# Near keys of the maximum pass: two units of 128-query windows become one unit of 64-query halves in four 64x64 tiles of the array

## The reference, cut to what matters

```python
def _strided_allowed(S):
    i = jnp.arange(S)[:, None]
    j = jnp.arange(S)[None, :]
    return (j % STRIDE == 0) | (jnp.abs(i - j) <= LOCAL)      # STRIDE 4, LOCAL 8
...
scores = jnp.einsum('bhqd,bhkd->bhqk', q, k) / jnp.sqrt(D)
scores = jnp.where(allowed, scores, -jnp.inf)
attn = jax.nn.softmax(scores, axis=-1)
out = jnp.einsum('bhqk,bhkd->bhqd', attn, v)
```

## Time and profile before

| what | value |
|---|---|
| median of 3 runs | 1088.07 us (1084.07 to 1089.80) |
| profiled execution, own time | 1086.01 us |
| its span, first to last instruction | 1084.2 us |
| PE / DVE / ACT / POOL busy | 95% / 86% / 77% / 23% of the span |
| mean granted clock of TensorE | 0.987 |
| chain that ended last | PE 76%, DVE 12%, issue 7% |

### The profile page before, as it was taken

The page is one execution under the profiler, slowest core; times in us unless marked ns, Lnnn a source line. Parts: engine busy times, 40 slices in busy tenths (PEclk is TensorE's granted clock), DMA queues, the critical chain, the costliest instruction groups (busy, mean ns, idle before and its releaser), DMA issues.

```text
span 1084.2 us, 27687 instructions
## 1 busy us (share of the span) xinstructions
PE 1028.3 (95%) x10694; PEld 462.7 (43%) x10695; DVE 933.8 (86%) x1162; ACT 839.8 (77%) x1590; POOL 251.2 (23%) x387
## 2 busy tenths in 40 slices
PE   4999999699999999999999999999999999999898
PEld 2666666233333333333333333333333333333487
DVE  6989897889999999999999999999999999999133
ACT  4667674288888888888888888888888888888600
POOL 2444453012212121221212122212121222212100
PEclk9999999599999999999999999999999999999999
DMA  6787878213223333333333333323343332231166
GB/s 197 227 254 252 262 250 274 54 46 88 85 83 90 98 85 93 102 91 99 97 96 109 98 99 95 104 84 108 91 113 88 105 91 82 86 85 58 48 236 239
DMA packets 166777, 134.07 MB, mean 124 GB/s; under 512 B 70492, under 2 KB 145884, under 8 KB 166636
## 3 DMA queue, kind: packets, MB, share of 16 engines
q1 hardware_dynamic: 163912, 128.06, 39.3%
q10 hardware_dynamic: 2736, 4.26, 1.2%
HBM read 71.13 MB, written 59.84 MB: 121 GB/s over the span
## 4 chain that ended last, share of the span: by engine, by line
PE 76%; DVE 12%; issue 7%; DMA 2%; ACT 2%; DVEq 0%; ACTq 0%
PE ps_attend L1228 17%; PE ps_attend L1145 12%; DVE peak_far L1087 10%; PE ps_attend L1186 10%; PE ps_project L621 7%; PE ps_attend L1235 6%; PE ps_attend L1308 5%; PE ps_attend L1156 4%; PE ps_project L679 4%; PE ps_attend L1197 3%; PE ps_project L594 3%; PE ps_attend L1163 3%; PE ps_attend L1204 2%; DMA sums<-out_rows 2%; PE ps_project L656 1%
## 5 line engine op out<-in xcount | busy, mean ns | idle before, releaser
L1087 DVE TENSOR_REDUCE peak_far<-ps_attend 128x2 f32<-128x1024 f32 x512 | 608.5, 1220 | 41.0 <-PE ps_attend L1186 30.8
L1028 ACT ACTIVATE probs<-ps_attend 128x512 f32<-128x512 f32 x1024 | 541.1, 597 | 49.5 <-PE ps_attend L1145 46.3
L1228 PE MATMUL ps_attend<-probs,v_op 128*17 128x512 f32 x2048 | 270.1, 600 | 0.5 <-issue 0.5
L1145 PE MATMUL ps_attend<-q_op,k_op 51*128 51x512 f16 x1024 | 252.1, 387 | 4.9 <-ACT probs L1028 3.3
L1186 PE MATMUL ps_attend<-k_op,q_op 48*128 48x512 f16 x1024 | 189.6, 388 | 26.1 <-DVE peak_far L1087 15.5
L1033 ACT ACTIVATE probs<-ps_attend 108x512 f32<-108x512 f32 x256 | 138.7, 594 | 34.6 <-PE ps_attend L1163 34.6
L1145 PEld LDWEIGHTS ps_attend<-q_op,k_op 51*128 51x128 f16 x1024 | 76.8, 93 | 193.9 <-ACT probs L1028 137.4
L894 POOL CAST negmax<-peak 128x16 bf16<-128x16 f32 x64 | 12.6, 196 | 609.6 <-DVE peak L1070 609.6
L1090 DVE TENSOR_REDUCE peak_near<-ps_attend 128x8 f32<-128x864 f32 x128 | 131.0, 1023 | 10.5 <-PE ps_attend L1204 10.4
L885 POOL TENSOR_TENSOR out_rows<-out_rows,share_rows 128x512 f32<-128x512 f32 x64 | 81.4, 1272 | 66.1 <-DMA share_rows<-shares_dram 64.0
L621 PE MATMUL ps_project<-xT_parts,w_parts 128*128 128x512 f16 x384 | 90.6, 387 | 2.1 <-DVE xT_parts L465 2.1
(11 more groups left out here) (91 smaller groups left out, 937.4 us busy)
## 6 DMA issues: line engine op xcount, KB each, us to landing
share_rows<-shares_dram SPq DMA_DIRECT2D x64, 256.0 KB
attn_dram<-out_rows SPq DMA_DIRECT2D x64, 256.0 KB, 5.5
q_dram<-qk_parts SPq DMA_DIRECT2D x48, 256.0 KB, 4.7
k_dram<-qk_parts SPq DMA_DIRECT2D x48, 256.0 KB, 2.7
q_op<-q_dram SPq DMA_DIRECT2D x128, 96.0 KB, 2.4
k_op<-k_dram SPq DMA_DIRECT2D x64, 144.0 KB, 3.1
v_dram<-v_sb SPq DMA_DIRECT2D x16, 544.0 KB, 3.0
base<-in_x SPq DMA_DIRECT2D x16, 512.0 KB, 4.7
```

The lines of the kernel that those rows point to most:

```text
L1028: ins = nc.scalar.activation(probs[:, r, h], ps_s[st.bank(kind)], ACT.Exp, scale=undo)
L1087: ins = nc.vector.tensor_reduce(peak_far[:, :, p, tile], banks, AX_X, ALU.max)
L1145: nc.tensor.matmul(bank, k[half(f, KM), keys], q[half(f, KM), p], start=True, stop=True).then_inc(s_ready, 1)
L1228: ins = nc.tensor.matmul(ps_o[h * VW:h * VW + VR], v[:, r, h * VR:(h + 1) * VR], probs[:, r, h], start=(r == 0), stop=False)
```

## The change

The two near units of a step become one. Its queries come in halves of 64 and each half meets its own window of 60 keys. The two heads of a pair use the upper and lower rows of the array and the two halves of a tile its left and right columns, so four 64x64 tiles are in use. One mask, relative to the query, serves every window: per tile of the array one product of 480 columns (2 pairs x 4 tiles x 60 keys), then 32 products of 64 x 60. One DVE maximum reads 960 elements per partition and gives 16. A step has nine units; the near unit stands seventh, on PE between `maxima()` and `far(3, 1)`.

As the mask no longer knows the ends of the sequence, a window that reaches past an end must find keys there that are allowed anyway: the strided keys of the two pairs now lie side by side in the middle of `k_op`, and the 6 columns at either end get copies of strided keys from POOL, four small copies for every load of keys (`set_edges`), which PE's near unit waits for in the step before their first use. The memsets of the ends and SP's wait for them go; SP loads two new mask arrays (128x64 and 128x480 bf16) at the start. `places(u)` and `strided(u)` give the new columns.

```diff
+SUB = HALF
+NEAR = (SUB + 2 * LOCAL) // STRIDE * (STRIDE - 1)
+SUB_STEP = SUB // STRIDE * (STRIDE - 1)
+NEAR_BANDS = ((1, 16), (4, 6), (12, 5))
...
+def strided(u):
+
+    return WPAD + (S if u else S - NS)
+
+
+def places(u):
+
+    return WPAD + u * (S + NS)
...
-        at = WPAD + u * S
-        eng.dma_start(k_op[half(f), at:at + S - NS].rearrange("r (c s) -> r c s", c=CPB), rows[:, :, ns:]
-                      ).then_inc(loaded, 16)
-        eng.dma_start(k_op[half(f), at + S - NS:at + S].rearrange("r (c s) -> r c s", c=CPB), rows[:, :, 0:ns]
-                      ).then_inc(loaded, 16)
+        eng.dma_start(k_op[half(f), places(u):places(u) + S - NS].rearrange("r (c s) -> r c s", c=CPB),
+                      rows[:, :, ns:]).then_inc(loaded, 16)
+        eng.dma_start(k_op[half(f), strided(u):strided(u) + NS].rearrange("r (c s) -> r c s", c=CPB),
+                      rows[:, :, 0:ns]).then_inc(loaded, 16)
...
-            sp.wait_ge(pads_set, 4)
+            sp.dma_start(keep["near_q"][:], io["rel_q"].bitcast(BF16)).then_inc(keep["bands_loaded"], 16)
+            sp.dma_start(keep["near_k"][:], io["rel_k"].bitcast(BF16)).then_inc(keep["bands_loaded"], 16)
...
-            for par in range(2):
-                nc.gpsimd.memset(keep["k_op"][par][:, 0:WPAD], 0.0).then_inc(pads_set, 1)
-                nc.gpsimd.memset(keep["k_op"][par][:, SK - WPAD:], 0.0).then_inc(pads_set, 1)
...
-UNITS = TT * PAIRS + TT // 2
+UNITS = TT * PAIRS + 1
...
-AHEAD = 5
-TURN = 8
+AHEAD = 4
+TURN = 7
...
-    ("far", 2, 1), ("far", 1, 0), ("far", 0, 0), ("near", 0), ("far", 2, 0),
-    ("far", 3, 1), ("far", 1, 1), ("far", 3, 0), ("near", 1), ("far", 0, 1),
+    ("far", 2, 1), ("far", 1, 0), ("far", 0, 0), ("far", 2, 0),
+    ("far", 3, 1), ("far", 1, 1), ("near",), ("far", 3, 0), ("far", 0, 1),
...
     def window(p, tile):
-        return p * S + WSTEP * tile
-
-    def strided(p):
-        return WPAD + p * S + S - NS
+        return places(p) - WPAD + WSTEP * tile
...
+        def set_edges(st):
+
+            k, it = k_op[st.parity(2)], st.iteration(2)
+            pool.wait_ge(k_loaded[st.parity(2)], 16 * 2 * 2 * PAIRS * (st.half_iteration(2) + 1))
+            edges = ((0, strided(0)), (SK - WPAD, strided(1)))
+            for i, (f, (to, of)) in enumerate(itertools.product(range(2), edges)):
+                nc.gpsimd.tensor_copy(k[half(f), to:to + WPAD], k[half(f), of:of + WPAD]).then_inc(edges_ready, 1)
+                pool.wait_ge(edges_ready, 4 * it + i + 1)
+
+        pool.wait_ge(done["y8_ready"], B * CPB)
+        set_edges(Step(0, FIRST))
         pool.wait_ge(done["base_ready"], B * CPB)
-        pool.wait_ge(pads_set, 5)
+        pool.wait_ge(pads_set, 1)
...
+            if st.n >= 0 and st.exists(2) and st.queries(2) == 0:
+                pool.wait_ge(negmax_ready, st.at(2))
+                set_edges(st)
...
-                    tile = 2 * kind[1]
-                    ins = nc.vector.tensor_reduce(peak_near[:, :, tile:tile + 2].rearrange("q f t p -> q f (t p)"),
-                                                  banks[:, :, 0:2 * PAIRS * WIN].rearrange("q f (g w) -> q f g w",
-                                                                                           w=WIN), AX_X, ALU.max)
+                    ins = nc.vector.tensor_reduce(peak_near[:].rearrange("q f p t -> q f (p t)"),
+                                                  banks[:, :, 0:PAIRS * TT * NEAR].rearrange(
+                                                      "q f (g w) -> q f g w", w=NEAR), AX_X, ALU.max)
...
+            if st.queries(2) == 0:
+                pe.wait_ge(edges_ready, 4 * (st.iteration(2) + 1))
             if 2 * n + 2 > U_BANKS:
                 pe.wait_ge(u_used, 2 * n + 2 - U_BANKS)
-            for t in range(2):
-                tile = 2 * kind[1] + t
-                cols = slice(tile * P, (tile + 1) * P)
-                at_mask = close(st.queries(d) * TT + tile)
-                whole = slice(t * PAIRS * WIN, (t + 1) * PAIRS * WIN)
-                for f in range(2):
-                    nc.tensor.matmul(banks[f][:, whole].rearrange("q (p w) -> q p w", p=PAIRS),
-                                     mask_q[half(f), st.queries(d) * CH + tile * P:st.queries(d) * CH + (tile + 1) * P],
-                                     mask_k[half(f), at_mask:at_mask + WIN].unsqueeze(1).broadcast_to([KR, PAIRS, WIN]),
-                                     start=True, stop=False)
-                for p in range(PAIRS):
-                    at = window(p, st.queries(d) * TT + tile)
-                    for f in range(2):
-                        ins = nc.tensor.matmul(banks[f][:, (t * PAIRS + p) * WIN:(t * PAIRS + p + 1) * WIN],
-                                               q[half(f), p, cols], k[half(f), at:at + WIN],
-                                               start=False, stop=(p == PAIRS - 1))
-                        if t == 1 and p == PAIRS - 1:
-                            ins.then_inc(u_ready, 1)
+            for sub, f in itertools.product(range(2), range(2)):
+                nc.tensor.matmul(banks[f][half(sub, SUB), 0:PAIRS * TT * NEAR], near_q[half(f)], near_k[half(f)],
+                                 start=True, stop=False)
+            for p, t in itertools.product(range(PAIRS), range(TT)):
+                for sub, f in itertools.product(range(2), range(2)):
+                    at = window(p, st.queries(2) * TT + t) + sub * SUB_STEP
+                    to = (p * TT + t) * NEAR
+                    ins = nc.tensor.matmul(banks[f][half(sub, SUB), to:to + NEAR],
+                                           q[half(f), p, t * P + sub * SUB:t * P + (sub + 1) * SUB],
+                                           k[half(f), at:at + NEAR], start=False,
+                                           stop=(p == PAIRS - 1 and t == TT - 1))
+                    if p == PAIRS - 1 and t == TT - 1 and sub == 1:
+                        ins.then_inc(u_ready, 1)
...
             far(2, 1)
             weigh_last(3)
             far(1, 0)
-            near_unit(0)
             far_unit(2, 0)
             far(1, 1)
             weigh_last(4)
@@ -1285,9 +1304,9 @@
             far(2, 0)
             weigh_own(0)
             maxima()
+            near_unit()
             far(3, 1)
             far_unit(3, 0)
-            near_unit(1)
             far(3, 0)
             weigh_own(1)
...
+    at = np.arange(NEAR)
+    hot = np.concatenate([np.arange(n)[:, None] == at // size % n for size, n in NEAR_BANDS])
+    beside = np.abs(STRIDE * (at // 3) + 1 + at % 3 - LOCAL - np.arange(SUB)[:, None]) <= LOCAL
+    rel_k = np.zeros((2, HALF, PAIRS * TT, NEAR), np.float32)
+    rel_k[:, :len(hot)] = hot[:, None, :]
+    rel_q = np.zeros((2, HALF, SUB), np.float32)
+    rel_q[:, :len(hot)] = np.where(hot.astype(int) @ beside.T.astype(int), 0, -BIG)
```

More of the change, by code:

```diff
@@ L690, in tensor_project @@
             chunks(pe, body)
-        done = dict(f_ready=f_ready, lo_ready=lo_ready, ranges_ready=ranges_ready, v_copied=v_copied,
+        done = dict(f_ready=f_ready, y8_ready=y8_ready, lo_ready=lo_ready, ranges_ready=ranges_ready, v_copied=v_copied,
                     base_ready=base_ready, bias_ready=bias_ready, masks_ready=masks_ready, rest_loaded=rest_loaded,
@@ L815, in part_attend @@
     k_loaded = keep["k_loaded"]
+    near_q, near_k = keep["near_q"], keep["near_k"]
+    edges_ready = sem("edges_ready")
     v_loaded = [sem(f"v_loaded{i}") for i in range(2)]
@@ L1069, in maximum @@
                     dve.wait_ge(negmax_ready, st.at())
-                nc.vector.tensor_tensor(peak[:, (st.n + 1) % 2], peak_far[:],
-                                        peak_near[:].rearrange("q f t p -> q f p t"), ALU.max).then_inc(peak_ready, 1)
+                nc.vector.tensor_tensor(peak[:, (st.n + 1) % 2], peak_far[:], peak_near[:], ALU.max
+                                        ).then_inc(peak_ready, 1)
             for i, kind in enumerate(MAXIMA):
@@ L1244, in far_unit, with near_unit @@
                 unit(st, ("far", tile, p))
-            def near_unit(tiles):
-                unit(st, ("near", tiles))
+            def near_unit():
+                unit(st, ("near",))
             def far(r, p):
@@ L1311, in project @@
             last.then_inc(y_ready, 1)
-        pe.wait_ge(keep["bands_loaded"], 16 * 6)
-        pe.wait_ge(pads_set, 5)
+        pe.wait_ge(keep["bands_loaded"], 16 * 8)
+        pe.wait_ge(pads_set, 1)
         pe.wait_ge(done["masks_ready"], 1)
@@ L1353, in build @@
             "k_op": [sb(f"k_op{i}", [P, SK], F16) for i in range(2)],
+            "near_q": sb("near_q", [P, SUB], BF16),
+            "near_k": sb("near_k", [P, PAIRS * TT * NEAR], BF16),
             "v_op": sb("v_op0", [P, NS // P + S // P, HG * VR]),
@@ L1358, in build @@
             "peak_far": sb("peak_far", [P, 2, PAIRS, TT]),
-            "peak_near": sb("peak_near", [P, 2, TT, PAIRS]),
+            "peak_near": sb("peak_near", [P, 2, PAIRS, TT]),
```

(2 more changed lines are left out.)

## The result

The changed kernel takes 1114.36 us (median of 4 runs, 1114.15 to 1114.96); the kernel before, beside it, 1087.28 us. The ratio is 1.0252, 95% interval 1.0223 to 1.028: slower by 2.5%. The profiled execution took 1114.96 us, its span is 1113.1 us, 28.9 more than before.

The account below looks back on a forecast made before the run. The prediction took a closed chain of PE and ACT's read latency to bound the step, 12.59 us. From 1086.0 us, + 37.2 for the near unit, - 1 lead-in, - 2 irregular steps gave 1120 us, range 1108 to 1152.

Parts of the forecast that it names:

- a chain of PE and ACT's latency: Attend stage: PE, ACT's read and PE again set the 12.59 us step; near-unit and DVE work are not on it.
- the last step: End of the attend stage: a step without units or DVE maxima took 12.58 us and should keep that length.
- The near unit: On PE between the negated maxima and far(3, 1): adds 0.60 us in each of 62 steps, 37.2 us.
- the burst of starts in the earlier trace: PE before the change: four matmuls of 0.28 us end within 0.30, eight weight loads of 0.09 within 0.13.
- the upper end of 1.2: Near unit's longest estimate: 72 instructions at the rate of 64 in 1.00 us are 1.12, with the switch 1.2 us.
- A: Near unit on PE: issue or pairwise tiles make it 0.94 to 1.2 us; 1151 us at 1.1; chance 0.27.
- D: Near unit on PE: the four tiles do not overlap at all, unit 1.7 us, kernel 1188 us; chance 0.03.
- the lead-in: Two steps at the start where maxima follow one another directly: 0 to 1.8 us saved, taken as 1.
- the irregular steps: Steps where DVE waited for row sums and held PE's next unit back: 0 to 7 us saved, taken as 2.
- The copies: POOL's copies of strided keys, in 15 of 62 steps: done at about 612.4, PE needs them at 613.00, no stall.
- Rival C: At the near unit's new place PE already waits for POOL's negated maxima: no difference, 1083 to 1090 us; chance 0.03.

Follow-up runs that it names:

- the unit in the gap: Changed kernel with its near unit between far(1, 0) and far(1, 1), far units moved later, sums turned ahead of the last unit: 1078.86 us, ratio 0.9929.

## Why the prediction was right

**The limit.** The prediction named a chain of PE and ACT's latency, and the units and DVE as no links of it. The gaps after the change, the last step and the experiments with columns, places and DVE all bear this out. No run changed ACT's read itself; that it ends the wait rests on the marks of the timeline. The same 0.58 us of PE cost 36 us at one place, of which 7.6 came back elsewhere, and nothing at another.

**The near unit.** I took 0.60 us, from 0.54 by its parts. It is 0.58: masks 0.23 (I had 0.20), and 0.35 from the first product to `far(3, 1)`. Eight rounds of four products at 0.032 are 0.25 of that (I had 0.24); what is left, 0.10, I put down to the change of shape (0.10). The forecast rested on the burst of starts in the earlier trace rows, against the upper end of 1.2, and the burst was the better guide. Rivals A and D, a slow stream and tiles that don't overlap, fall by this row.

The 32 products start within 0.42 - 0.19 = 0.23 us (the group less the mean length of one), on average 7 ns apart. By the Trainium skill, "TensorE: Matmul & The Clock Gate", Part 1, starts are never less than about 25 ns apart. As one floor for all tiles together the trace contradicts that. For one tile it doesn't: the four products of a round, one in each tile, start some 3 ns apart, and the next round follows after 32 ns.

**The sum.** From first to last negated maxima it is now 832.9 us:

```profile
L1159 PE MATMUL ps_attend<-ident_bf,negmax x64: 229/230/288, 202.8 to 1035.6; 128*128 128x128 bf16 x64
```

Against 804.2 before that is 28.7 more. The median of the 63 intervals went from 12.588 to 13.174 us. 62 of them have the unit at its new place; 62 times the difference of 0.586 are 36.3 (I had 62 x 0.60 = 37.2), so 7.6 us came back. The first two intervals, the lead-in, stood 4.7 us over the median and the later ones 6.5; now it is 2.7 and 0.3. The first interval lies ahead of the 62 and gets no 0.586, so the lead-in gave 1.4 (4.7 less 2.7 and 0.6; I had 1), the irregular steps 6.2 (I had 2, with an upper end of 7). All three terms were off in the same direction, so nothing cancelled. The last is the one that I mis-sized: it carries 4.2 of the 5.5 us by which the sum's 34.2 exceeds the 28.7 of these two traces. The measured 1114.4 us lies inside the range of 1108 to 1152.

Its step said that most of a delay by late sums "finds the same order behind it"; in the changed kernel nearly all of it is gone. There DVE waits for sums 3 times instead of 11, but late sums alone don't explain it. Without the copies the same steps have four late sums of 0.2 to 0.7 us, and yet stand only 0.4 us over the median. With the old unit at the new place (median step 12.97, DVE's work as before) six sums are late, and the later steps stand 2.7 over it, not 6.5. With the unit in the gap (old step, lighter DVE, sums inverted later) it is 1.6. So the longer step absorbs most of what late sums do. How much of the rest is the lighter DVE no run separates.

**The copies.** I expected them to end 0.6 us before PE needs them; they do so 0.85 us before. Rival C, a hole at the new place, was not there.

**What the change could have brought.** DVE's 0.8 us a step were real and made no step shorter. With the unit where PE waits anyway the kernel takes 1078.9 us, 7.5 less than before; 3 us of that the kernel before gets from inverting its sums later.

## What to carry to other kernels

When three engines are each busy for nine tenths of a step, none of them need be the limit: lay out one step and see which starts wait for what, and look for a step in which one engine has nothing to do. If that step is as long as the others, work saved on that engine doesn't shorten the step; at most it calms irregular ones. A stretch of work is worth what its place makes it: ask of each place whether the engine waits there for something else, and how long, before asking how fast the new form is.

## What was not expected of the hardware

The stream of small products kept its pace: 36 loads and 36 products on four 64x64 tiles took 0.48 us (0.58 less 0.10 for the change of shape). 0.23 of it is four masks of 480 columns, which are 0.20 us for one, so the tiles ran side by side. Most of the loads of 64 columns stayed hidden: a round of four products takes 0.032 us, its 60 columns at 2.4 GHz 0.025.

And a change of the array's shape costs about the same 0.10 us in the three places that rows here show. Ahead of `weigh` the last product starts 0.31 to 0.32 before it, of which 512 columns are 0.21. Behind the negated maxima it is 0.16, of which 128 columns are 0.05. Ahead of the 64x64 unit a pair takes 0.33 us, and 0.23 where the next product has its own shape. The Trainium skill, "TensorEngine Tiling (Array Packing)", Key Properties, says that such a change drains the array. The trace agrees with a cost of that kind, but no run changes the shape alone.
